# Layer-1 weight preparation moved one step ahead of the FFN, its rest into the layernorm behind it

## What is computed

```python
xn = _layernorm(x)
x = x + L0_attn(xn) + L0_ffn(xn)          # Taylor-feature attention; FFN of 8 experts, top 1
xn = _layernorm(x)
x = x + L1_attn(xn) + L1_ffn(xn)          # softmax attention; FFN with ternary weights

# L0_ffn: every expert on every token, then the gate picks one
h1 = jnp.maximum(jnp.einsum('th,ehf->etf', xt, W1) + b1[:, None, :], 0.0)
ye = jnp.einsum('etf,efh->eth', h1, W2) + b2[:, None, :]
y = jnp.einsum('te,eth->th', onehot, ye) * gate[:, None]

# L1_ffn: weights are made ternary by their own mean absolute value
def _ternary(w):
    scale = jnp.maximum(jnp.mean(jnp.abs(w)), 1e-08)
    w_t = jnp.clip(jnp.round(w / scale), -1.0, 1.0)
```

## Time and profile before

| | us |
|---|---|
| timed runs | 8230.98 and 8677.65, median 8454.31 |
| the profiled execution, its own device time | 8078.13 |
| its span on the slowest core (core 5) | 8076.3 |
| spans of the 8 cores | 8035.1 to 8076.3 |
| mean granted TensorE clock of the cores | 0.844 to 0.845 |
| busy: TensorE / VectorE / ScalarE | 6018.2 / 2371.2 / 1742.8 |

### The profile page before, as it was taken

The page is one execution under the profiler, slowest core; times in us unless marked ns, Lnnn a source line. Parts: engine busy times, 40 slices in busy tenths (PEclk is TensorE's granted clock), DMA queues, the critical chain, the costliest instruction groups (busy, mean ns, idle before and its releaser), DMA issues.

```text
span 8076.3 us, 72400 instructions; the slowest of 8 cores (8035.1 to 8076.3 us)
## 1 busy us (share of the span) xinstructions
PE 6018.2 (75%) x25392; PEld 2488.6 (31%) x25392; DVE 2371.2 (29%) x4977; ACT 1742.8 (22%) x2768; POOL 152.3 (2%) x177
## 2 busy tenths in 40 slices
PE   3354899999997886887888888726755666676687
PEld 1111344443443333333333333312211122222333
DVE  4633222222222222222222222347253423223000
ACT  1000111111111111111111111100043456474121
POOL 0000000000000000000000000000000000000000
PEclk9555899999998998998999989858867677777898
DMA  1000323323413113113112121120102020201423
GB/s 51 5 0 1 59 52 63 60 37 76 84 42 65 37 37 73 37 32 58 29 38 49 29 58 29 33 74 11 42 15 32 1 32 1 32 1 16 133 63 81
DMA packets 165181, 336.80 MB, mean 42 GB/s; under 512 B 13171, under 2 KB 54940, under 8 KB 162404
## 3 DMA queue, kind: packets, MB, share of 16 engines
q0 software_dynamic: 107888, 221.31, 15.6%
q1 hardware_dynamic: 56948, 110.85, 4.4%
HBM read 445.96 MB, written 46.14 MB: 61 GB/s over the span
## 4 chain that ended last, share of the span: by engine, by line
PE 64%; DMA 11%; DVE 10%; ACT 6%; issue 6%; DVEq 3%; SPq 0%; POOL 0%; ACTq 0%; POOLq 0%
PE pA L706 22%; PE pB L722 11%; PE pC L722 11%; ACT expT L1091 4%; PE pA L1210 3%; DMA wbuf<-L_W 3%; DMA denM<-den_stg 2%; DMA w1t_sc<-buf 2%; PE pB L1224 1%; PE pC L1224 1%; PE pD L620 1%; PE pC L1113 1%; PE pA L1082 1%; DVE zT L1128 1%; DVE den_stg L1125 1%
## 5 line engine op out<-in xcount | busy, mean ns | idle before, releaser
L706 PE MATMUL pA<-xnT,W1q 128*128 128x512 bf16 x8192 | 1821.0, 384 | 0.0
L711 ACT ACTIVATE h<-pA,b1c 128x512 bf16<-128x512 f32 x1024 | 705.3, 689 | 3611.3 <-PE pA L706 3611.3
L706 PEld LDWEIGHTS pA<-xnT,W1q 128*128 128x128 bf16 x8192 | 808.7, 99 | 986.1 <-issue 47.6
L736 DVE SCALAR_TENSOR_TENSOR acc<-pB,G,acc 128x512 f32<-128x512 f32 x512 | 383.3, 750 | 2238.7 <-PE pB L722 1639.8
L722 PE MATMUL pB<-W2q,h 128*128 128x512 bf16 x4096 | 938.4, 379 | 127.5 <-ACT h L711 120.2
L722 PE MATMUL pC<-W2q,h 128*128 128x512 bf16 x4096 | 937.6, 379 | 0.0
L722 PEld LDWEIGHTS pB<-W2q,h 128*128 128x128 bf16 x4096 | 383.7, 98 | 641.7 <-issue 212.4
L1091 ACT ACTIVATE expT<-pA,shcol 128x512 bf16<-128x512 f32 (+1 forms) x704 | 462.2, 735 | 422.8 <-PE pA L1082 362.2
L736 DVE SCALAR_TENSOR_TENSOR acc<-pC,G,acc 128x512 f32<-128x512 f32 x512 | 383.9, 751 | 539.6 <-PE pC L722 348.6
L722 PEld LDWEIGHTS pC<-W2q,h 128*128 128x128 bf16 x4096 | 390.1, 98 | 482.3 <-issue 29.0
L1098 DVE TENSOR_TENSOR expT<-expT,s_masks 128x512 bf16<-128x512 bf16 (+1 forms) x640 | 269.8, 424 | 819.3 <-ACT expT L1091 798.1
(11 more groups left out here) (253 smaller groups left out, 3616.0 us busy)
## 6 DMA issues: line engine op xcount, KB each, us to landing
W1q<-L_W POOLq DMA_DIRECT2D x32, 2048.0 KB, 18.9
W2q<-L_W POOLq DMA_DIRECT2D x32, 2048.0 KB, 32.8
wbuf<-L_W SPq DMA_DIRECT2D x32, 1024.0 KB, 12.2
w2tb<-w2t_sc POOLq DMA_DIRECT2D x8, 4096.0 KB, 17.3
wbuf<-L_W SPq DMA_DIRECT2D x32, 512.0 KB, 10.6
wbuf<-L_W SPq DMA_DIRECT2D x64, 256.0 KB, 5.7
WOb<-L_WO POOLq DMA_DIRECT2D x8, 2048.0 KB, 15.8
o<-stg POOLq DMA_DIRECT2D x64, 256.0 KB, 4.1
```

Source lines behind the costliest of these rows:

```text
L706: t_p1 = mm.mark(TE.raw.matmul(PS[bk], lhsT=W1q[:, s, a, ft * 128:(ft + 1) * 128], rhs=xnT[:, a, tq * 512:(tq + 1) * 512], start=(a == 0), ...
L711: bank_free[bk] = sc.mark(SE.raw.activation(h1[:, ft, :], PS[bk], ACT.Relu, bias=b1c0[:, e, qq * 8 + ft:qq * 8 + ft + 1]))
L736: bank_free[bk] = vv.mark(VE.raw.scalar_tensor_tensor(out=aslc, in0=PS[bk], scalar=G[:, tq * 4 + ts_, e:e + 1], in1=aslc, op0=OP.mult, op1 ...
```

## The change

One step of the generator is run before `l0_ffn` begins, so ahead of the router; `l0_ffn` still calls it twice after each pass, but returns the generator in place of running it out; the second layernorm calls it once after the two sums of each tile, until it ends. The generator's buffers are now allocated before those of the FFN and freed after the layernorm.

```diff
-            def layernorm_phase(want_s, S_full):
+            def layernorm_phase(want_s, S_full, gen=None):
...
                         t_sq_rd[sl] = vv.mark(VE.raw.tensor_reduce(
                             cols[:, 1, i:i + 1], sq_t[:, sl, :], AX, OP.add))
+                        if gen is not None and next(gen, "END") == "END":
+                            gen = None
...
+                    if gen is not None:
+                        for _ in gen:
+                            pass
                     barrier()
...
                         t_b2use[sl] = mm.tok()
-                    if tern_gen is not None:
-                        for _ in tern_gen:
-                            pass
                     barrier()
-
-            def tern_steps():
-                st = ExitStack()
+                    return tern_gen
+
+            def tern_steps(st):
...
                 tk["tern"] = t_st
-                st.close()
...
+            tern_left = None
+            st_tern = ExitStack()
             if upto >= 3:
-                l0_ffn(tern_steps() if upto >= 4 else None)
+                g_tern = tern_steps(st_tern) if upto >= 4 else None
+                if g_tern is not None:
+                    next(g_tern)
+                tern_left = l0_ffn(g_tern)
...
-                layernorm_phase(False, None)
+                layernorm_phase(False, None, tern_left)
+                st_tern.close()
```

More of the change, by code:

```diff
@@ L1264, in _ @@
                                       deps=(vv.tok(), mm.tok(), sc.tok())))
+            if upto < 5 and tern_left is not None:
+                for _ in tern_left:
+                    pass
+            if upto < 5:
+                st_tern.close()
             if upto >= 5:
-                layernorm_phase(False, None)
+                layernorm_phase(False, None, tern_left)
+                st_tern.close()
                 if "xnT" in dbg_aps:
```

## The result

| | before | after |
|---|---|---|
| median of the timed runs, us | 8317.97 (20 runs, 8069.84 to 8830.87) | 8300.37 (21 runs, 7988.67 to 8825.18) |
| ratio of the runs that can be compared | | 0.9914, interval 0.9891 to 0.9937 |
| span of the profiled execution, slowest core | 8076.3 (core 5) | 7994.8 (core 2) |
| after less before, each core against itself | | -71 to -90, mean -81.6 |

The change makes the kernel 0.86% faster. That is small, but more than three times what the interval leaves open (0.23% to either side). Some executions of either kernel run at a lower clock on one die and take some per cent longer; the ratio leaves them out, the medians have them in, and so the medians differ by only 17.6 us.

The account below looks back on a forecast made before the run. Layer-0 FFN taken as bound by TensorE's matmuls, with gains where TensorE stands still. Terms 7.0 + 1.5 - 45.5 - 27.8 = -64.8 us, off the two-run median 8454.31, gave 8389.5 us; range 8000 to 8500.

Parts of the forecast that it names:

- Step 0 ahead of the router: Before the router: the generator's first step, sums of absolute values, delays pass 0 to 869.0; +7.0 us, bounds 0 to 12.
- W1's boundaries: Stretches after passes 11 to 19: eight full store waits instead of seven, 301.4 us against 299.9; +1.5 us.
- W2's boundaries: Stretches after passes 20 to 30: store ends each pair, 15.0 us per boundary, 159.5 in place of 205.0; -45.5 us.
- Rival A: W2 boundaries: loads stay as late as behind the store, 22.1 us each; +6.2 us in all, 8460.5; chance 0.12.
- rival C: W2 boundaries: loads come as fast as alone, 9.5 us each; sum -119.8 us, 8334.5; chance 0.05.
- Run-out and layernorm: After pass 31: one pair, then eight steps between layernorm's reduces, 96.4 us in place of 124.2; -27.8 us.
- Rival B: Layernorm pays each step in full: 127.1 us, part +2.9, sum -34.1 us, 8420.2; chance 0.12.
- The clock: TensorE's granted clock in W1 and W2 boundaries: still falls to the lower level with shorter boundaries; cost nothing.
- Sum: Whole kernel: the four terms for early step, W1, W2, and run-out with layernorm together; -64.8 us.
- same: Whole kernel: measured time stays within 2% (169 us) of the time before; chance 0.87.

Follow-up runs that it names:

- the first two-buffer kernel: Kernel before, with leftover steps moved into layernorm, old pairing, plus two ternary buffers and two store semaphores; fastest run 7923.71 us against 8072.51, no ratio.

## Why the prediction came out as it did

The mechanism was the forecast one, and the saving in microseconds came close. The point (8389.5) was wrong, by the last step of the sum. That the median after lies inside the range says little, since the range is 500 us wide and the saving was 82. By its own steps:

- *Step 0 ahead of the router, +7.0*: pass 0 starts at 869.1 on core 5 (forecast 869.0), at 865.8 to 871.6 over the cores. The reduces wait for their loads as said. That the router's start and not the weights sets pass 0 is shown by the fixed distance between the two, above. On core 2, whose router starts 2.9 us later than forecast, pass 0 starts at 871.6.

The router there, first the two reduces and then the router's own, answering to the earlier trace rows:

```profile
833.52 1.22 DVE L811 TENSOR_REDUCE redc<-wbuf 128x1 f32<-128x1024 f32 x1 [5.28 <-DMA wbuf<-L_W]
...
835.30 1.22 DVE L811 TENSOR_REDUCE redc<-wbuf 128x1 f32<-128x1024 f32 x1 [0.55 <-DMA wbuf<-L_W]
...
836.44 0.15 DVE L656 TENSOR_REDUCE colsr<-pD 128x1 f32<-128x8 f32 x1
```

- *W1's boundaries, +1.5 (301.4)*: 299.00. The first one took 9.80 (forecast 9.2), the eight others 36.2 on this core and 35.6 over all cores (forecast 36.5).
- *W2's boundaries, -45.5 (159.5)*: 153.15, so -51.9. The mean of those with weights beside them is 14.1 over the cores, against 15.0. After pass 22 the parts are 5.8, 7.9 and 0.9 as forecast, without the 0.4 for the shared queue; but 7.9 is at the upper end: after passes 20 to 29 the fourth load of core 2 landed after 7.0 to 8.7 us, about 7.5 in the median, where I had taken 7.9, the median of the third load before, and 0.4 on top. The last boundary took 9.36 (forecast 9.5). Rival A (22.1) and rival C (9.5 everywhere) are out: A by the landings, and the first two-buffer kernel shows that A's landing is about right where the store does stand ahead (15.6 to 17.6 on core 5, A took 15.4); C by the kernel without weights, which gives 9.4 to 10.0 only when their transfer is gone.

That the load stood behind the store's bytes can be seen in the packets of the kernel before: between the store's issue at 3802.99 and its landing there is a stretch, 3810 to 3814, in which SP's queue (`q1`) moves 305 packets, all under 2 KB. A store to `w2t_sc` has rows of 1 KB, a load into `wbuf` rows of 2 KB, so all 305 are the store's.

```profile
DMA packets 609, 0.93 MB, mean 234 GB/s; under 512 B 0, under 2 KB 305, under 8 KB 609
...
q1 hardware_dynamic: 305, 0.31, 28.1%
```

The rule of the Trainium skill that each DMA engine consumes a ring's descriptors in order ("DMA: Bandwidth & Descriptors", section "Queues, rings and completion order") agrees with this, and with the landings: the load behind the store landed at 3823.5 against 3821.4, though no group waited for that store.

- *Run-out and layernorm, -27.8 (96.4)*: 15.44 + 81.91 = 97.35, so -26.9. The store's stall of VectorE was 2.4 us, not 2.0, at three of the eight steps. Rival B (127.1) is out.
- *The clock, costed at nothing*: the cores' mean granted clock is 0.847 to 0.851, where it was 0.844 to 0.845, and the passes themselves take 1.8 us less in all, in the mean of the cores.
- *Sum*: forecast -64.8. The parts above set core 2 after against core 5 before, as the forecast did. Each core against itself, in the mean of the eight, the four parts are +7.1, -0.6, -52.5 and -27.4, together -73.4; with the passes the cores are 75.2 us earlier at the end of the layernorm's sums. So the term most off in the sum is W2's, -45.5 for -52.5, because its loads land sooner than I took. The spans differ by 81.6: the remaining 6.4 (from +4.2 to -18.0 by core) lies behind the sums, in stretches where no instruction changed, and stays unexplained. In per cent of the profiled execution the forecast was -0.80, and the measured ratio is -0.86, with -0.80 inside its interval.

The step that failed is the one from the sum to the time: the saving was taken off a median of two runs, 8454.31, and the median of twenty runs of the same kernel is 8317.97. So the point, 8389.5, lies not only 1.1% above the median after but 0.9% above that of the kernel before: as a time it names a slower kernel, though the sum beneath it says faster. The profiled execution (8078.13) lay within 0.1% of the fastest run of before (8069.84), and 8013.3, its footing less the saving, is 0.3% from the fastest run after (7988.67). The other failure is the statement that about 2% is what a measurement can tell from no change: the ratio is known to 0.23% either way. The change is within 2%, as the chance of 0.87 said, but a forecast of -0.80% from terms that each could be bounded should have been called a small gain and not mainly "same".

## What to carry to other kernels

When filler work (here the weight preparation) makes the engine that bounds the kernel wait, what counts is how much of the main work lies between two of its steps: the same preparation, spread in small steps over the chunks rather than in pairs behind the passes, gave 6.7% where the better pairing gave 0.9%. The store issued ahead of a load in the same queue delayed that load even where nobody waited for the store, so before adding a buffer see which of two overlapping waits is next. And take a saving worked out in microseconds off the profiled execution, not off the median of a few scattered runs.

## What the runs showed of the hardware

- The time of one 256 KB load on SP's queue depends on its neighbours: 2.7 us alone; 7.4 to 9.8 beside the weights' transfer on POOL's queue in the boundaries before, 7.0 to 9.1 in those after (core 2); 13.6 to 15.7 with a 512 KB store ahead of it as well in the boundaries before (core 5), 15.6 to 17.6 in those of the first two-buffer kernel (core 5).
- Taking the wait for the store away did not shorten the boundary, and on some cores it grew (core 5: 23.0 to 24.8 against 20.8 to 23.0). The store then is issued between two loads as before, and on core 5 lands after 13.6 to 15.8 us in place of 11.9 to 14.0. Why the transfers are slower there stays open.
- The eight W1 stores that TensorE waited for cost it 22 us each (178.2 over 8), those of W2 in the layernorm 6.3 (25.3 over 4), for the same 512 KB; VectorE's work ahead of the store is in both. The stores alone, on core 2, landed after 16.8 to 20.2 us when issued within a W1 boundary, beside the weights' transfer, and after 2.9 to 3.2 in the layernorm. Without the weights' transfers W1's stores landed after 3.5 to 6.5 (core 0), so it is that transfer that makes them slow.
